# Six-column batches with own and shared slots, paced transfers and one-hots over a column's run, in the message-passing layer of a graph network

## The reference

```
in_agg = segment_sum(edge_feat, dst); out_agg = segment_sum(edge_feat, src)
h = relu(concat([in_agg, out_agg, x]) @ W1 + b1)          # 192 -> 256
y = x + (h @ W2 + b2)                                      # 256 -> 64
out = (y - mean(y)) / sqrt(var(y) + eps)
```

## Time and profile before

| | |
|---|---|
| median of 3 runs | 1434.02 us (1429.0 to 1435.78) |
| profiled execution | 1431.8 us, its span 1430.0 us |
| busy: PE, DVE, POOL, ACT | 1345.7, 1350.9, 1154.9, 1009.2 us |
| mean granted clock of TensorE | 0.984 |
| slot store of a chunk (slot_tiles<-slots_out) | x78, 1018.5 KB each |
| feature load (feat<-in_edge_attr) | x195, 256.0 KB each |

### The profile page before, as it was taken

One profiled execution on the slowest core, in us unless ns is written; L12 is line 12 of the kernel. 1 busy time (PEld: TensorE's weight loads), 2 busy tenths in 40 slices (PEclk: granted clock), 3 DMA queues, 4 the chain that ended last, 5 costly groups with the idle time before them and its releaser, 6 DMA issues.

```text
span 1430.0 us, 63740 instructions
## 1 busy us (share of the span) xinstructions
PE 1345.7 (94%) x23675; PEld 1055.1 (74%) x23675; DVE 1350.9 (94%) x3463; ACT 1009.2 (71%) x2185; POOL 1154.9 (81%) x663
## 2 busy tenths in 40 slices
PE   3559999999999999999999899999999999999896
PEld 2349999999999999999999566566666666566543
DVE  6989999999999999999999999999999999998586
ACT  6528888878888888888778666766776667676443
POOL 3888888888888888888888888888888888888633
PEclk9969999999999999999999999999999999999998
DMA  9327777787777777778888777777767777767541
GB/s 300 46 16 191 191 190 190 191 190 193 196 196 196 194 193 193 196 197 219 218 216 219 186 188 196 185 183 186 181 171 186 187 181 208 166 155 181 97 134 43
DMA packets 216557, 255.41 MB, mean 179 GB/s; under 512 B 99251, under 2 KB 179220, under 8 KB 216214
## 3 DMA queue, kind: packets, MB, share of 16 engines
q1 hardware_dynamic: 123880, 223.88, 49.1%
q0 software_dynamic: 92384, 28.77, 22.4%
q10 hardware_dynamic: 144, 0.67, 0.2%
HBM read 143.18 MB, written 110.08 MB: 177 GB/s over the span
## 4 chain that ended last, share of the span: by engine, by line
PE 51%; DMA 17%; POOL 15%; issue 10%; DVE 6%; ACT 0%; DVEq 0%; POOLq 0%; SPq 0%; ACTq 0%
PE psum L1580 21%; PE psum L1603 19%; DMA out_tables<-payload,target 16%; POOL out_tables L711 15%; PE psum L1557 3%; PE psum L1564 2%; PE psum L1643 1%; PE psum L1776 1%; PE psum L1641 1%; PE psum L1767 1%; PE psum L1788 1%; DMA rows_i<-in_dst 1%; DVE from_group L1072 1%; DVE same L1260 1%; DVE in_group L1109 1%
## 5 line engine op out<-in xcount | busy, mean ns | idle before, releaser
L711 POOL DMA_INDIRECT out_tables<-payload,target x628 | 1121.5, 1786 | 209.7 <-issue 186.3
L1580 PE MATMUL psum<-parts,to_slot 128*128 128x194 bf16 x6552 | 587.2, 248 | 0.2 <-ACT slots_out L806 0.2
L1580 PEld LDWEIGHTS psum<-parts,to_slot 128*128 128x128 bf16 x6552 | 553.7, 98 | 16.3 <-issue 0.4
L1603 PE MATMUL psum<-to_node,slots_in 64*64 64x448 bf16 x9828 | 480.8, 351 | 4.8 <-DVE to_node L1233 4.0
L1603 PEld LDWEIGHTS psum<-to_node,slots_in 64*64 64x64 bf16 x9828 | 283.7, 107 | 180.0 <-issue 5.6
L806 ACT ACTIVATE slots_out<-psum 128x388 bf16<-128x388 f32 (+1 forms) x936 | 366.4, 472 | 55.3 <-PE psum L1580 47.2
L1194 DVE TENSOR_SCALAR to_slot<-iota_h,slot 128x896 bf16<-128x896 f16 x936 | 381.9, 460 | 0.1
L1233 DVE TENSOR_SCALAR to_node<-iota_h,slot_rel 128x448 bf16<-128x448 f16 x819 | 268.6, 346 | 0.8 <-PE psum L1603 0.5
L1233 DVE TENSOR_SCALAR to_node<-iota_rows,slot_rel 128x448 bf16<-128x448 f16 x546 | 236.7, 434 | 0.0
L867 ACT ACTIVATE to_node<-apart 128x448 bf16<-128x448 bf16 x273 | 149.0, 573 | 67.2 <-PE psum L1603 66.5
L830 ACT ACTIVATE payload<-psum 128x256 f32<-128x256 f32 x157 | 60.2, 383 | 180.3 <-PE psum L1643 176.3
(11 more groups left out here) (127 smaller groups left out, 771.6 us busy)
## 6 DMA issues: line engine op xcount, KB each, us to landing
slot_tiles<-slots_out SPq DMA_DIRECT2D x78, 1018.5 KB
feat<-in_edge_attr SPq DMA_DIRECT2D x195, 256.0 KB
slots_in<-slot_tiles SPq DMA_DIRECT2D x40, 970.0 KB
slots_in<-slot_tiles SPq DMA_DIRECT2D x40, 921.5 KB
out_tables<-payload,target POOLq DMA_INDIRECT x628
out_tables<-zeros POOLq DMA_DIRECT2D x4, 1600.0 KB
feat<-out_tables SPq DMA_DIRECT2D x48, 128.0 KB, 2.2
slots_in<-slot_tiles SPq DMA_DIRECT2D x14, 242.5 KB
```

What stands on the lines that cost most here:

```text
L711: e.indirect_dma_start(out_tab, at, payload[b][:, t, :], None, element_offset=k * TABLE_ROWS * D, compute_op=ALU.add).then_inc(s_tab[k], 16)
L1580: last = e.matmul(ps_share[r % BANKS][:, o:o + SLOT_W], to_slot[m][:, k, g * P:(g + 1) * P], parts[b][:, SHARE_FROM + MINI * m + k, 1:], s ...
L1603: return e.matmul(ps_groups[g % 2][h][cols, 0:HOT], slots_in[p % RING][rows, j - PART_FROM[p], D * k:D * (k + 1)], to_node[rows, node_buf( ...
```

## The change

- A batch has six columns instead of four, and a chunk two batches instead of three (MINI, MINIS). There are 22 groups of 286 nodes, 11 tiles a batch, and 1716 tiles in all.
- Of a group's 64 slots in a batch, eight belong to each column and 16 are shared (HOMES, SHARED). A column reaches only the tiles with its own and the shared slots; the one-hots of sharing cover only that run, 528 to 624 slots. Tiles 0 to 7 take products of 1, 2, 2, 1, 2, 2, 2 and 1 columns, tiles 8 to 10 of all six. The one-hots of summing have 286 columns.
- The first 4 chunks are early, the last 16 sum. ranks(n) runs between early chunks and has another form.
- The window of receivers is 48 wide.
- The feature loads of a sharing chunk wait for slot evictions (FEAT_ROUNDS), the slot store is three DMAs (STORES), and a slot load is four (load_tiles), since own and shared slots lie apart in HBM.
- x is transposed in the last 13 summing chunks (x_turned), and the products of x for the first two groups stand ahead of the tail.
- In a sharing chunk PE, DVE and ACT have another order.

```diff
-WINDOW = P // HALVES
+WINDOW = 48
...
-FIRST = 2
-MINIS = 3
-MINI = 4
+FIRST = 4
+MINIS = 2
+MINI = 6
 SHARE = MINIS * MINI
 SHARE_FROM = COLS - SHARE
 SLOTS = P // 2
-GROUP_NODES = 448
+GROUP_NODES = 286
 SLOT_GROUPS = -(-N_NODES // GROUP_NODES)
 NODE_PAIRS = SLOT_GROUPS // 2
 PAIR_NODES = 2 * GROUP_NODES
-SLOT_COLS = SLOT_GROUPS * SLOTS
+HOMES = (8,) * MINI
+SHARED = SLOTS - sum(HOMES)
+HOME_AT = [SLOT_GROUPS * sum(HOMES[:k]) for k in range(MINI + 1)]
+SHARED_TILE = HOME_AT[MINI] // P
+COLUMN_TILES, HOME_FIRST, SHARED_FIRST, USED_FROM, USED = [], [], [], [], []
+for k in range(MINI):
+    home = [t for t in range(HOME_AT[k] // P, (HOME_AT[k + 1] - 1) // P + 1) if t < SHARED_TILE]
+    together = list(range(SHARED_TILE, NODE_PAIRS))
+    own, others = HOME_AT[k] - P * home[0], HOME_AT[MINI] - P * SHARED_TILE
+    homes_ahead = (P * len(home + together) - own, home + together, own, own, P * len(home) + others)
+    shared_ahead = (P * len(together) + own + HOMES[k] * SLOT_GROUPS - others, together + home, others, P * len(together) + own, others)
+    width, tiles, start, own_at, shared_at = homes_ahead if own + HOMES[k] * SLOT_GROUPS > P * len(home) else min(homes_ahead, shared_ahead)
+    COLUMN_TILES.append(tiles)
+    USED_FROM.append(start)
+    USED.append(width)
+    HOME_FIRST.append(own_at - start)
+    SHARED_FIRST.append(shared_at - start)
+COLUMN_SLOTS = [P * len(tiles) for tiles in COLUMN_TILES]
+COLUMN_FROM = [sum(COLUMN_SLOTS[:k]) for k in range(MINI + 1)]
+WIDEST = max(USED)
+TILE_COLUMNS = [[(k, tiles.index(t)) for k, tiles in enumerate(COLUMN_TILES) if t in tiles] for t in range(NODE_PAIRS)]
 HOT = GROUP_NODES
-HOT_ROW = 64
-SUMS = 18
+HOT_ROW = 26
+SUMS = 16
 SHARE_CHUNKS = N_CHUNKS - FIRST - SUMS
 SHARE_PAIRS = SHARE_CHUNKS // 2
 TILES = SHARE_CHUNKS * MINIS
 ALL_TILES = NODE_PAIRS * TILES
 FIRST_TILES = 20
-LAST_TILES = 150
+LAST_TILES = TILES
 LEAD = 12
-GROUP_ENDS = ((3, 3), (6, 0), (8, 3), (11, 0), (13, 3), (16, 1))
...
-PARTS = 3 * RING
+PARTS = 2 * RING
 PART_FROM = [TILES * k // PARTS for k in range(PARTS + 1)]
-PIECES = 4
+PIECES = 2
+LOADS = MINI // 2 + 1
...
+        STORES = ((0, 4), (4, 8), (8, NODE_PAIRS))
+        FEAT_ROUNDS = (2, 4)
         CHUNK_ROUNDS = MINIS * ROUNDS
-        HEAD_ROUNDS = CHUNK_ROUNDS // 2
+        HEAD_ROUNDS = ROUNDS
+        FIRST_ROUNDS = 2
         BANKS = len(ps_share)
-        assert CHUNK_ROUNDS == MINIS * QUADS and ROUNDS % BANKS == 0
+        assert CHUNK_ROUNDS % BANKS == 0
...
+                    if at is not None:
+                        e.wait_ge(s_slot_ev, CHUNK_ROUNDS * at + FEAT_ROUNDS[h] + BANKS)
...
+            def load_tiles(g, p, a, z):
+                lo = PART_FROM[p]
+                into = slots_in[p % RING][:, a - lo:z - lo, :].rearrange("p t w -> p (t w)")
+                homes = slot_rows[0:HOME_AT[MINI], :].rearrange("(k r) w -> r k w", k=MINI)
+                both, shared = 2 * HOMES[0], 2 * SHARED
+                for j in range(LOADS - 1):
+                    e.dma_start(into[j:P:LOADS, :], homes[both * g:both * (g + 1), 2 * j:2 * j + 2, a * SLOT_W:z * SLOT_W]
+                                ).then_inc(s_slot_in[p % RING], 16)
+                at = HOME_AT[MINI] + shared * g
+                e.dma_start(into[LOADS - 1:P:LOADS, :], slot_rows[at:at + shared, a * SLOT_W:z * SLOT_W]
+                            ).then_inc(s_slot_in[p % RING], 16)
...
+                    for a, z in STORES:
+                        e.wait_ge(s_slot_ev, CHUNK_ROUNDS * at + ROUNDS * (MINIS - 1) + -(-z // 2) + BANKS)
+                        e.dma_start(slot_tab[a:z, :, bass.ds(at * (MINIS * SLOT_W), MINIS * SLOT_W)].rearrange("g p w -> p g w"),
+                                    slots_out[b][:, a:z, :, :].rearrange("p g m w -> p g (m w)")).then_inc(s_slot_out[b], 16)
...
+            def sharing_chunk(c, i, b, mode, s):
+                split_hi(i + b, c + 1, 1 - b)
+                payload_quad(c, b, mode, 0)
+                put_nodes(s + 1, 1 - b)
+                slots(i, s, b, range(0, ROUNDS))
+                split_mid(c + 1, 1 - b)
+                slots(i, s, b, range(ROUNDS, CHUNK_ROUNDS))
...
+            def out_of_transposes(g):
+                e.wait_ge(s_xt, g + 1)
+                n = tiles_in(g)
+                rows, turns = D * min(n, 2), (n + 1) // 2
+                e.activation(xT[g][0:rows, :], ps_turned[0:rows, 0:turns * P], ACT.Copy).then_inc(s_cat, 1)
...
-                    last = e.tensor_scalar(to_slot[m][:, k, :], iota_h[:, :],
+                    at = COLUMN_FROM[k] + USED_FROM[k]
+                    last = e.tensor_scalar(to_slot[m][:, at:at + USED[k]], iota_h[:, 0:USED[k]],
...
+            def ranks(n):
+                e.wait_ge(s_pre, PRE_GROUPS[n])
+                for k in range(MINI):
                     for g in range(SLOT_GROUPS):
+                        last = e.matmul(ps_counts[:, k, g, :], in_group[:, k, g, :], ones_bf[:, 0:2], start=True, stop=True)
+                last.then_inc(s_counts, 1)
+                e.wait_ge(s_pre, PRE_EARLIER[n])
+                for k in range(MINI):
+                    for a, (g, w) in enumerate(RANK_BANKS):
+                        turn = len(RANK_BANKS) * (MINI * n + k) + a
+                        if turn >= len(RANK_BANKS):
+                            e.wait_ge(s_first, turn - len(RANK_BANKS) + 1)
+                        for j in range(w):
+                            to = ps_ranks[a][:, BATCH_TILES * j:BATCH_TILES * (j + 1)]
+                            last = e.matmul(to, above_bf[:, :], in_group[:, k, g + j, :], start=True, stop=(k == 0))
+                            if k > 0:
+                                last = e.matmul(to, earlier_bf[0:BATCH_TILES, k, g + j:g + j + 1].to_broadcast([BATCH_TILES, P]),
+                                                ident_64[0:BATCH_TILES, 0:BATCH_TILES], start=False, stop=True)
+                        last.then_inc(s_ranks, 1)
+                for g in range(SLOT_GROUPS):
+                    last = e.matmul(ps_group, ident_bf[:, :], from_group[:, :, g, :], start=(g == 0), stop=(g == SLOT_GROUPS - 1))
+                last.then_inc(s_group, 1)
+                e.wait_ge(s_masked, MINI * (n + 1))
+                for g in range(SLOT_GROUPS):
+                    last = e.matmul(ps_found, ident_h[:, :], place[:, :, g, :], start=(g == 0), stop=(g == SLOT_GROUPS - 1))
+                last.then_inc(s_placed, 1)
+                e.wait_ge(s_pre, PRE_SLOTS[n])
+                if n == BATCHES_OF_RANKS - 1:
+                    e.matmul(ps_over, ones[0:BATCH_TILES, :], over[0:BATCH_TILES, :], start=True, stop=True).then_inc(s_over, 1)
+                spread(FIRST // BATCHES_OF_RANKS * (n + 1), 0, 0)
...
+                    columns = TILE_COLUMNS[g]
+                    for k, t in columns:
+                        last = e.matmul(ps_share[r % BANKS][:, o:o + SLOT_W], to_slot[m][:, COLUMN_FROM[k] + t * P:COLUMN_FROM[k] + (t + 1) * P],
+                                        parts[b][:, SHARE_FROM + MINI * m + k, 1:], start=((k, t) == columns[0]),
+                                        stop=((k, t) == columns[-1]))
...
+            def x_turned(g, evicted):
+                if g == 0:
+                    e.wait_ge(s_x, 32)
+                n = tiles_in(g)
+                sides, turns = min(n, 2), (n + 1) // 2
+                e.wait_ge(s_ev, evicted)
+                for k in range(turns):
+                    last = e.transpose(ps_turned[0:D * sides, k:turns * P:turns],
+                                       tile_cols(xs, g, n)[:, 2 * k:2 * k + sides, :].rearrange("p t d -> p (t d)"), ident)
+                last.then_inc(s_xt, 1)
...
             def sharing_head(s, b):
                 c = s + FIRST
                 e.wait_ge(s_lo, c + 1)
+                for r in range(0, FIRST_ROUNDS):
+                    slot_round(s, b, r)
                 payload_quad(c, b, c, SHARING, 0)
-                for r in range(0, HEAD_ROUNDS):
+                for r in range(FIRST_ROUNDS, HEAD_ROUNDS):
                     slot_round(s, b, r)
             def sharing_tail(s, b):
                 c = s + FIRST
-                for r in range(HEAD_ROUNDS, CHUNK_ROUNDS - MINIS):
+                sum_windows(c, b)
+                for r in range(HEAD_ROUNDS, CHUNK_ROUNDS - 3):
                     slot_round(s, b, r)
                 spread(c + 1, 0, 0)
-                for r in range(CHUNK_ROUNDS - MINIS, CHUNK_ROUNDS):
+                for r in range(CHUNK_ROUNDS - 3, CHUNK_ROUNDS):
                     slot_round(s, b, r)
-                sum_windows(c, b)
```

499 lines of the change are left out of this document (239 added, 260 removed).

## The result

The changed kernel takes 1367.42 us (median of 4 runs, 1364.15 to 1375.19) beside 1434.78 of the kernel before: a ratio of 0.9546, 95% interval 0.9497 to 0.9595. I had predicted 1394, in a range from 1338 to 1446. The experiments ran on three chips, each used once. Two of them took 1478 to 1479 us for the kernel before, and one of these two was also given the changed kernel, which took 1483; the third took 1437 for the kernel before. Kernels are compared within one of the two, some of them across two chips; where that matters the text gives both times and ratios to the kernel before on the same chip.

What follows compares the result with a forecast made beforehand. Sharing was taken as bound by the PE, ACT and four-bank loop, summing by POOL. 190 + 632 + 2 + 5.5 + 486 + 75 = 1390.5 us of span, so 1394 us against 1434.0; range 1338 to 1446.

Steps and rivals of the forecast that it cites:

- Early stage: Everything before the first sharing chunk: two more early chunks and two rank batches of 57 us; 190 us for 99.4.
- Sharing: 78 chunks at 8.1 us, 8.0 from the loop and 0.1 for POOL and DMA: 632 us.
- The stall ahead of round 4: In each sharing chunk PE stands until ACT, behind hi split and payload, evicts round 0: 1.03 us.
- Rival (1): Sharing: the banks cover the stall if ACT runs ahead; period 7.5 us, 1347 us in all; chance 0.20.
- Rival (2): Sharing: shorter but equally dense one-hots stretch scatters as before; period stays 8.74 us, 1444 us in all; chance 0.10.
- Rival (3): Sharing: DMA packets limit, with load 8.0 us and share at most 0.88; chunk 9.1 us, 1472 us; chance 0.12.
- Summing: Summing ends by POOL: 252 scatters at 1.93 us take 486 us, bounds 469 and 495; PE needs 373.
- rival (4): Summing: short products stay at 0.048 us, so PE needs 550 us for 486; 1458 us in all; chance 0.04.
- Tail: After summing: x transposes and two groups of own products leave it, 5 us off; 75 us for 80.
- At nothing: Sharing's waiting feature loads, slot loads as four DMAs and stores in three parts were booked at no cost.

Runs made afterwards that it cites:

- hi_late: Changed kernel with ScalarE's first two slot evictions and payload ahead of the next chunk's hi split: 1432.48 us, ratio 0.9699, beside the changed kernel's 1483.35.
- share3: Changed kernel without the fourth column's scatter in each of the 78 sharing chunks, its sums left out: 1480.35 us, ratio 1.0029.
- hi_late3: hi_late with the one-hots of two more columns ahead of the split of the rest on VectorE, targets staying behind it: 1484.4 us, ratio 1.0343.
- wide_hot: Changed kernel with the sharing one-hots written over a column's whole tiles, 661 columns on average for 563: 1387.48 us, ratio 0.9653.
- two_parts: Changed kernel without the products of the slots' lowest third in summing, 6864 sum products for 10296: 1375.24 us, ratio 0.9587.

## Why the prediction held, term by term

The time lies in the range, and the two stages that make most of it came out for the reasons given. That the sum is only 23 us off is not luck of terms that cancel: nearly all of it is one term, the early stage. But the forecast holds for the first conditions alone. In the second the changed kernel took 1483 us, above the range, and was no faster than the kernel before, which the forecast had at 0.11; nothing in it allowed for the engines issuing later.

**Early stage: the mis-sized term.** 190 predicted, 162.6 measured: 27 us too much, where the whole sum of the span, 1390.5, is 23 above the 1367.2 measured (sharing, summing and the tail together fall 4 short). A batch of ranks takes 43.2 us (48.99 to 92.2) where I had 57.2. The step that failed is the price of PE's small products. The 132 counting products I priced at the 0.105 us of 14 that weigh 117 columns; they have 78 columns and take 0.068 (54.56, 8.96 us), which is 0.105 x 78/117, the scaling that I gave the 242 rank products and not these: 4.8 us. The rank products begin 0.065 apart, near my 0.063, at first (67.17, 67.24) and 0.038 from 71.4 us on (76.09, 76.13), after PE had worked without a break from 65.63 on (the granted clock is given as 1.00 for both stretches, so no row shows what changed); with the last eviction and mask they end at 79.10, 13.5 us for 16.8. The 44 products of 468 columns take 0.20 us each, 8.9 in all for 12, and 2 us of these lie beside the last mask: 7.07 behind it. The small VectorE steps take 6.0 for 7.

**Sharing.** 632 + 2 + 5.5 predicted, 640.9 measured; 8.1 a chunk predicted, 8.16 on average and 8.07 in the middle of the stage. The stall ahead of round 4 is at the place and of the size worked out: counted from the end of PE's last round, about 464.75, ACT's hi split starts at 0.44 (0.41 predicted), the payload at 1.39 (1.37), eviction 0 at 2.00 (2.0), and round 4 at 2.56 (2.55). ACT's order is its cause (hi_late), and scatters less don't shorten it (share3), both shown in the second conditions. That POOL was level with it I had as 0.1 us; how little room that leaves, hi_late3 and wide_hot showed. Rival (1), that ACT would run ahead, failed in the kernel as it stands. Rival (2), POOL at its old pace, failed here: a scatter takes 1.72 us on average, within my 1.6 to 1.8. In the three kernels with a shorter loop POOL did become what stopped it. Rival (3) said that a DMA share of 0.88 was the limit: it is 1.00 from 163 to 800 us, above the 0.9 that I had said would prove me wrong, and the chunk is 8.07 all the same. The busy share had no limit at 0.88, and it isn't the bound: the waits for DMA in 500 us are 8.5 us, all POOL's, and in hi_late3 chunks of the same transfers follow each other at 7.7 and 7.79 us. (With the terms given, the load by packets would have been 7.1 + 1.76 = 8.9 and not 8.7.) The 9.06 of the second conditions is near this rival's 9.1 by chance: with the same transfers hi_late takes 8.46 there.

**Summing.** 486 predicted for 252 scatters at 1.93, 484.7 measured at 1.92, held by POOL in the first conditions (two_parts). The price of PE's products, 0.031 by columns, is 0.034, and rival (4) failed. But I had PE at 373 us of 486, and there it stands with gaps that I hadn't seen coming; in the first conditions they fit into its room (two_parts).

**Tail.** 75 predicted, 79.0 measured. I took off 5 us for the 25 x transposes and the two groups that left it. PE's busy time went down by 2.2 us (59.9 for the 62.1 of the earlier trace rows) and the tail by 1.6. PE does set the pace of most of it (it is busy 49.2 of the 50 us from 1303 to 1353), so the place was right and the size wrong: two x transposes held PE for 0.27 us a group (1387.18 to 1387.45 before), and a group takes 4.66 us (1321.21 to 1325.87) for 4.80 (1383.09 to 1387.89). And 1.5 us went back at the start, where the first eight products of the sums take 5.77 us for 4.25, at a granted clock of 0.70 (1296 to 1303) for 0.88 (1358 to 1364).

**At nothing.** The pacing was not nothing in the second conditions, 19 us. I had written that a load is needed only some 5 us later and that each us of a late one is a chunk's; without the pacing loads do come late in the last twenty chunks (6.7 us of ACT's waiting). What it is worth in the first conditions isn't shown.

**Open.** Why the second conditions issue more slowly, whether that belongs to the chip or to the hour (none of the three chips was used twice), and what the kernel before loses there stage by stage; what holds summing there; whether hi_late, some 50 us better in the second conditions, is a gain in the first, where POOL has no room at 8.07; whether 14 summing chunks are one there. The narrower window, the shape of a batch and the x products were not taken out one by one, so the gain is not divided among them.
